# One LSTM step in TensorE's banks: input and bias rows injected behind the cell, twelve steps written out

## What the reference computes

```python
g0 = x[:, 0] @ W_ih[0].T + b_ih[0] + b_hh[0]
h, c = _lstm_activate(g0, c0)
def step(carry, x_t):
    h, c = carry
    sel_in = jnp.concatenate([h, c, x_t], axis=-1)
    logits = sel_in @ W_sel.T + b_sel
    onehot = jax.nn.one_hot(jnp.argmax(logits, axis=-1), Sx)
    g_all = einsum('bi,sgi->bsg', x_t, W_ih) + einsum('bh,sgh->bsg', h, W_hh) + b_ih + b_hh
    g = einsum('bsg,bs->bg', g_all, onehot)
    h2, c2 = _lstm_activate(g, c)      # sigmoid(f)*c + sigmoid(i)*tanh(g); sigmoid(o)*tanh(c2)
    return ((h2, c2), h2)
```

## Time and profile before

| | us |
|---|---|
| device time, median of 3 runs | 6272.86 (6269.54 to 6273.96) |
| the profiled execution, device time | 6278.15 |
| its span, first to last instruction | 6276.3 |
| PE busy | 5392.8 (86%) |
| DVE busy | 3097.9 (49%) |
| ACT busy | 1088.6 (17%) |
| POOL busy | 612.9 (10%) |

### The profile page before, as it was taken

One profiled execution on the slowest core, in us unless ns is written; L12 is line 12 of the kernel. 1 busy time (PEld: TensorE's weight loads), 2 busy tenths in 40 slices (PEclk: granted clock), 3 DMA queues, 4 the chain that ended last, 5 costly groups with the idle time before them and its releaser, 6 DMA issues. The chain is left out here.

```text
span 6276.3 us, 214043 instructions
## 1 busy us (share of the span) xinstructions
PE 5392.8 (86%) x84948; PEld 3269.5 (52%) x84948; DVE 3097.9 (49%) x13265; ACT 1088.6 (17%) x4645; POOL 612.9 (10%) x1014
## 2 busy tenths in 40 slices
PE   8998778849998929999999999999999999977778
PEld 6643443314666615555555555555555555544444
DVE  4401443214552165555555555555555555564543
ACT  0000000002331131111111111111111111122312
POOL 0000660002650000000000000000000000011100
PEclk9999998979999969999999999999999999989877
DMA  0000111467432330000000000000000000000010
GB/s 10 21 30 11 39 44 44 97 136 253 119 105 100 139 123 5 5 5 10 5 5 5 10 5 5 5 5 10 5 5 5 5 10 0 0 24 37 23 55 9
DMA packets 128787, 240.28 MB, mean 38 GB/s; under 512 B 47084, under 2 KB 64114, under 8 KB 127687
## 3 DMA queue, kind: packets, MB, share of 16 engines
q1 hardware_dynamic: 68584, 146.72, 6.6%
q0 software_dynamic: 60128, 92.58, 5.9%
HBM read 165.58 MB, written 73.29 MB: 38 GB/s over the span
## 5 line engine op out<-in xcount | busy, mean ns | idle before, releaser
L1456 PE MATMUL bank<-lstm_w,step_h_parts 128*32 128x128 f16 (+1 forms) x59904 | 1233.0, 238 | 172.1 <-issue 164.0
L1456 PEld LDWEIGHTS bank<-lstm_w,step_h_parts 128*32 128x32 f16 x59904 | 1116.8, 97 | 488.4 <-issue 478.0
L1427 PE MATMUL bank<-lstm_w 128*128 128x512 f16 x4992 | 1297.0, 383 | 3.2 <-issue 3.2
L1480 DVE TRANSPOSE_TENSOR_REDUCE step_summed<-bank 128x4 f32<-128x128 f32 x1872 | 670.0, 358 | 292.7 <-PE bank L1456 285.6
L1427 PEld LDWEIGHTS bank<-lstm_w 128*128 128x128 f16 x4992 | 386.4, 98 | 388.5 <-issue 5.1
L1406 ACT ACTIVATE step_act_out<-step_gates 128x4 f32<-128x4 f32 x625 | 128.5, 206 | 2082.3 <-DVE step_gates L1486 2078.8
L1486 DVE SCALAR_TENSOR_TENSOR step_gates<-step_summed,lstm_inv_scale,step_xgs 128x4 f32<-128x4 f32 x1872 | 416.0, 222 | 68.7
L1530 DVE COPY step_xgs<-step_xg 128x16 f32 x624 | 109.2, 175 | 688.7 <-issue 664.5
L1396 POOL COPY xnT<-step_state 128x4 f32 (+1 forms) x625 | 116.4, 186 | 3170.0 <-DVE step_state L1513 3170.0
L1109 PE MATMUL bank<-sum_parts,sum_hot 125*125 125x512 f16 x1600 | 347.6, 381 | 6.9 <-DVE sum_parts L1068 6.9
L1437 PE MATMUL bank<-lstm_wsel,step_state 128*1 128x4 f32 x4992 | 214.9, 168 | 115.3 <-DVE step_state L1503 115.3
(11 more groups left out here) (368 smaller groups left out, 6578.2 us busy)
## 6 DMA issues: line engine op xcount, KB each, us to landing
rel_h<-rel_h_sb SPq DMA_DIRECT2D x39, 1024.0 KB, 4.3
lstm_xg<-xg_g POOLq DMA_DIRECT2D x4, 5000.0 KB, 19.5
step_xg<-lstm_xg SPq DMA_DIRECT2D x25, 800.0 KB, 4.4
xg_w<-in_c_w_ih SPq DMA_DIRECT2D x8, 2048.0 KB, 10.7
lstm_w<-in_c_w_hh SPq DMA_DIRECT2D x4, 4096.0 KB, 30.8
rel_z<-rel_z_sb POOLq DMA_DIRECT2D x8, 1250.0 KB, 22.9
rel_zg<-rel_z POOLq DMA_DIRECT2D x8, 1248.0 KB
cheb_w<-in_L_gnn_weight SPq DMA_DIRECT2D x8, 1024.0 KB
```

The lines of the kernel that those rows point to most:

```text
L1427: nc.tensor.matmul(idle[:], w[:, 0, 0, 0, 0, 0:128], w[:, 0, 0, 0, 0, :], start=True, stop=True)
L1456: last = nc.tensor.matmul(bank[32 * q:32 * q + 32, 0:32 * (end - first)], h_parts[:, c, :], w[:, s, c, q, a, 32 * first:32 * end], start=( ...
L1480: nc.vector.tensor_reduce(summed[:, first:end], bank[:, 0:32 * (end - first)].rearrange("p (b r) -> p b r", r=32), X_AXIS, ALU.add, apply_ ...
```

## The change

Five things change, all in the LSTM.

1. `lstm_inputs` turns its products round: x is stationary (125 rows of x at a time), and 512 weight columns move. Each of 16 groups (gate and quarter of the hidden size) times 5 row tiles gives 80 tiles. The result is split into three bfloat16 parts (ACT takes the high and middle one, DVE the rests) and stored as `lstm_xg` with a bank's layout: 128 columns for each of the four cells. The bias is not added, but split and stored in the same way (`lstm_bias`).
2. In the loop, `inject` puts the input and bias rows of all four cells into each of four gate banks with one bfloat16 product of 512 columns (128 stationary columns). It stands at the start of the next step, right behind the cell's code, and waits for DVE's sum of that bank.
3. The cell has four parts of 128 columns (f, g, i, o) in place of three. It adds to the 128 columns of its cell in the injected bank. `add_input`, the copy `step_xgs` and the four `WARM_GATES` products are gone. ACT applies the scale while it reads the sums.
4. PE's loop has 52 rounds of 12 steps written out, so that a step's slot in the ring of input rows is a constant. DVE, ACT and POOL still loop over single steps.
5. DVE's wait for a part is `_wait_ge(done, 1)` on the reduction itself; four decrements behind the pick (`parts_taken`) bring the semaphores back to zero.

```diff
-WARM_PICK, WARM_GATES = 4, 4
+WARM_PICK = 4
-CHUNK = 25
-RING = 3 * CHUNK
+XG_CHUNK = 4
+XG_SLOTS = 3
+XG_RING = XG_SLOTS * XG_CHUNK
...
-                    wt = w[:, n % 2, c, i % (GC // 2), :]
-                    nc.tensor.matmul(B.bank[2 * (i % 4)][:, 0:CUT], wt, xnT[:, c, 0:CUT], start=(c == 0),
-                                     stop=(c == KC - 1))
-                    last = nc.tensor.matmul(B.bank[2 * (i % 4) + 1][:, 0:N - CUT], wt, xnT[:, c, CUT:N],
+                    last = nc.tensor.matmul(B.bank[i % 6][0:R, :], xnT[:, c, m * R:(m + 1) * R], w[:, n % 2, c, :],
                                             start=(c == 0), stop=(c == KC - 1))
...
-                act.wait_ge(gates_f, n)
-                nc.scalar.activation(act_out[:, 0:4], gates[:, 0:4], ACT.Sigmoid).then_inc(sig_f, 1)
+                act.wait_ge(summed_f, n)
+                nc.scalar.activation(act_out[:, 0:4], summed[:, 0:4], ACT.Sigmoid, scale=L.inv[:, 0:1]
+                                     ).then_inc(sig_f, 1)
...
-            with pe.Fori(1, STEPS) as t:
...
+            def inject(part, at, stop):
+                p, bank, _, _ = part
+                return nc.tensor.matmul(bank[:], rows[:, p, :], xg[:, at, :], start=True, stop=stop)
+
+            def add_half(part, s, c, a, stop):
+                p, bank, _, _ = part
+                for q in range(4):
+                    last = nc.tensor.matmul(bank[32 * q:32 * q + 32, 128 * s:128 * s + 128], h_parts[:, c, :],
+                                            w[:, s, c, q, a, 128 * p:128 * p + 128], start=False, stop=stop,
+                                            tile_position=(0, 32 * q))
+                return last
...
+            def step(t, at):
+
+                if at % XG_CHUNK == 0:
+                    pe.wait_ge(xg_loaded[at // XG_CHUNK], 16)
+                    pe.sem_inc(xg_loaded[at // XG_CHUNK], -16)
+                for part in parts:
+                    pe.wait_ge(part[3], t)
+                    last = inject(part, at, stop=False)
+                last.then_inc(injected, 1)
...
-                keep_clock_up(WARM_GATES)
+            with pe.Fori(0, ROUNDS) as r:
+                for at in range(XG_RING):
+                    step(pe.snap(r * XG_RING + (at + 1)), at)
...
-            def add_input(part, t):
-                first, end, _, _, summed_part, gates_part = part
-                dve.wait_ge(summed_part, t)
-                nc.vector.scalar_tensor_tensor(out=gates[:, first:end], in0=summed[:, first:end],
...
+                nc.vector.tensor_reduce(summed[:, 4 * p:4 * p + 4], bank[:, bass.ds(s * 128, 128)].rearrange(
+                    "p (b r) -> p b r", r=32), X_AXIS, ALU.add, apply_transpose=True
+                                        )._wait_ge(done, 1).then_inc(summed_part, 1)
```

More of the change, by code:

```diff
@@ L1178, in _, with take_rest @@
+            for k in range(4):
+                pool.wait_ge(stored[k], 16 * (TILES // 4))
         @block.vector
         def _(dve):
[L1180 to L1190, removed]
+            def take_rest(i):
+                if i >= 4:
+                    dve.wait_ge(lo_ready, i - 3)
+                dve.wait_ge(hi_ready, i + 1)
+                nc.vector.tensor_tensor(rest[:, i % 4], B.bank[i % 6][0:R, :], parts[:, i % 4, 0], ALU.subtract
+                                        ).then_inc(rest_ready, 1)
@@ L1196, in _, with keep_hi @@
         def _(act):
[L1197 to L1205, removed]
+            def keep_hi(i):
+                if i >= 4:
+                    act.wait_ge(stored[i % 4], 16 * (i // 4))
+                act.wait_ge(done, i + 1)
+                nc.scalar.copy(parts[:, i % 4, 0], B.bank[i % 6][0:R, :]).then_inc(hi_ready, 1)
@@ new lines, in lstm_steps @@
+    xg_loaded = [sem(f"xg_loaded{k}") for k in range(XG_SLOTS)]
+    w = L.raw[:, 0:BLOCKS, :].bitcast(F16).rearrange("p (s c q) (a k) -> p s c q a k", s=CELLS, c=KC, a=2)
+    part_f = (0, B.bank[0], done_f, summed_f)
+    part_g = (1, B.bank[1], done_g, summed_g)
+    part_i = (2, B.bank[2], done_i, summed_i)
+    part_o = (3, B.bank[3], done_o, summed_o)
+    parts = (part_f, part_g, part_i, part_o)
+    score = B.bank[4][0:1, 0:8]
+    idle = B.bank[5]
+    halves = [(c, a) for c in range(KC) for a in range(2)]
@@ L1449, in _ @@
                 s = pe.value_load(pick[0:1, 0:1])
-                def cell(s):
-                    for first, end, bank, done, _, _ in parts:
-                        for c in range(KC):
-                            for a in range(2):
-                                for q in range(4):
-                                    last = nc.tensor.matmul(
-                                        bank[32 * q:32 * q + 32, 0:32 * (end - first)], h_parts[:, c, :],
-                                        w[:, s, c, q, a, 32 * first:32 * end],
-                                        start=(c == 0 and a == 0), stop=(c == KC - 1 and a == 1),
-                                        tile_position=(0, 32 * q))
-                        last.then_inc(done, 1)
                 with pe.If(s < 2):
@@ L1555, in _ @@
             dve.wait_ge(init, 1)
-            dve.wait_ge(xg_loaded, 16)
-            for first, end, _, _, _, gates_part in parts:
-                nc.vector.tensor_copy(gates[:, first:end], xg[:, 0, first:end]).then_inc(gates_part, 1)
-            forget(1)
-            new_i(1)
-            new_c(1)
-            weigh_h(1)
-            new_h(1)
-            choose(1)
-            with dve.Fori(1, STEPS - 1) as t:
-                finish(t, t + 1)
-                choose(t + 1)
-            finish(STEPS - 1, STEPS)
+            dve.wait_ge(rows_loaded, 16)
+            nc.vector.tensor_scalar(rows[:], rows_f[:], L.up[:, 0:1], None, ALU.mult).then_inc(rows_ready, 1)
+            finish(0, None, 1)
+            with dve.Fori(1, STEPS) as t:
+                s = choose(t)
+                finish(s, t, t + 1)
 def add_hidden(nc, ctx, B, L):
@@ L2290, in lay_out @@
         b = out.pop("L2_ffn_" + name).reshape(4, 4, 4, 4, 32)[:, order]
[L2291 removed]
+        out["c_" + name] = np.ascontiguousarray(b.transpose(1, 2, 0, 3, 4).reshape(16, 512))
+    rows = np.zeros((128, 4, 128), np.float32)
+    for n in range(16):
+        rows[3 * n:3 * n + 3, n // 4, 32 * (n % 4)] = 1.0
+        rows[64 + 3 * n:64 + 3 * n + 3, n // 4, 32 * (n % 4)] = 1.0
+    out["c_xg_rows"] = rows
     w = out.pop("L2_ffn_W_sel")
```

233 lines of the change are left out of this document (139 added, 94 removed).

## The result

| | before | changed |
|---|---|---|
| device time, median, us | 6271.5 (6269.54 to 6273.96, 4 runs) | 11404.88 (11396.54 to 11422.4, 4 runs) |
| profiled span, us | 6276.3 | 11420.6 |
| mean granted clock of PE | 0.944 | 0.705 |

The changed kernel takes 1.8189 times as long, 95% interval 1.8157 to 1.822. The forecast was 10,540 us with a range of 8,900 to 12,300: the measured time lies inside it, 865 us above its middle.

What follows compares the result with a forecast made beforehand. The PE-DVE-ACT ring of the LSTM loop was taken as the bound, every wait paid 624 times. Step 4.55 + code arrival 6.2 + clock 1.2 = 12.0 us against 5.165: +4265 us, 10,540 us, range 8,900 to 12,300.

Steps and rivals of the forecast that it cites:

- The bound and its price: PE's instruction blocks in the LSTM loop: an absent one can be used 3.4 us after it is asked for.
- Rival 2: In the twelve-step loop, code stays or always arrives in time: 4.55 us a step, 5,900 us; chance 5%.
- The waits by cell: Waits for code at jumps and block edges in PE's loop, summed for each cell: mean 6.2 us a step.
- The jump to cell 3: Branch to the last cell copy in PE's loop: one jump of 772 instructions, 3.4 us.
- The step without the code's arrival: One LSTM loop step if no code had to arrive: 4.5 to 4.6 us, where it was 5.165.
- The four injects [...] lie where PE waits anyway: Injects in PE's loop: as long as the four `WARM_GATES` products they replace, 1.04 us, and placed where PE waits.
- The gain of 0.6 us in the new c: In the LSTM step the new c can start at about 4006.75 instead of 4007.35: 0.6 us less.
- The clock: PE's granted clock in the loop: low for over half the time, adding 1.2 us a step, bounds 0 and 1.9.
- The input stage: `lstm_inputs`: 640 passes in 272 us against 269 before, booked at 0, bounds -20 and +100 us.
- Rival 1: PE asks for two or three blocks ahead: 9.3 and 7.7 us a step, 8,860 and 7,860 us; chance 9%.
- rival 4: Gain and waits in the loop cancel, needing a mean wait of 0.6 us a step; chance 1%.
- Rival 3: A jump's block queues behind the next one already asked for: 11,790 to 12,350 us; chance 3% beyond the range.

Runs made afterwards that it cites:

- run 1: The kernel before with PE's step written out twelve times and nothing else changed but the place of the four filler products: 10409.07 us.
- run 4: The changed kernel with one step in PE's loop, the ring's slot from a register and one semaphore counting SP's loads: 6470.8 us, ratio 1.0313.
- runs 2 and 3: The kernel before with PE's step written out two times (6.5 blocks) and three times (9.8 blocks): 6285.08 us, ratio 1.001, and 11292.85 us.
- Run 7: The changed kernel with the four copies of the cell in reverse order in the code, branches turned to match: 11552.29 us, ratio 1.8406.
- run 5: The kernel of run 4 with the injects behind the scores, in place of three of the four filler products: 6264.52 us, ratio 0.9985.
- run 8: The kernel of run 5 with DVE's MAX8 and MAX_INDEX at its turn's end, value load and decrements at the next one's start: 6009.2 us, ratio 0.9577.
- Run 9: The kernel of run 8 with 8 instead of 4 buffers for the stores of the input stage: 5986.9 us, ratio 0.954.

## Why the prediction was right, and by how much it was off

**The bound and its price.** Right. The reading of the earlier trace rows, one jump that took 3605 ns and one pause within a cell, was the whole effect in small: a block that is not there costs PE 3.3 to 3.9 us at most jumps (3.4 was taken), and q8 moved 2425 packets (over 2000 forecast), 3.8 a step without the 45 of before (3 to 4). One reading was inexact: the clock fell at 2315.5 us, inside the gap that ended at 2316.31, and not behind it.

**The cause.** Shown. The old step written out has it without the rest of the change (run 1), and the change without the writing out does not have it (run 4). Rival 2, that the code stays, had its point in question at a loop of 51 blocks; runs 2 and 3 put the limit between 6.5 and 9.8.

**The waits by cell.** The prediction's waits for each cell, with its 4.55 us for the step and 1.2 for the clock added (5.75), stand beside what was measured from pick to pick:

| cell | predicted | measured | off by |
|---|---|---|---|
| 0 | 4.2 + 5.75 = 9.95 | 10.79 | 0.84 |
| 1 | 6.6 + 5.75 = 12.35 | 13.20 | 0.85 |
| 2 | 8.2 + 5.75 = 13.95 | 14.85 | 0.90 |
| 3 | 6.0 + 5.75 = 11.75 | 15.24 | 3.49 |

Two steps of the working failed, and they can be told apart here.

*The jump to cell 3* was booked as one jump of 772 instructions, 3.4 us. It is two: L1519 goes to the compare L1525, which stands ahead of cell 2, and that block has to arrive only to say that the next jump goes to cell 3, which has to arrive too. In the trace the first takes 3.61 us and the second 3.36 in the mean of the 129. That is the 5.83 us of idle time ahead of cell 3 in the timeline. 3.49 less the 0.86 that the other cells are off by as well is 2.6 us, times 129/624 = 0.54 us a step. Run 7 confirms it: the cell that stands last pays it, whichever it is.

*The step without the code's arrival* was booked at 4.55 us. Run 4 measured 5.43, and the 0.88 between them is what the other cells are off by. Both faults together, 0.88 + 0.54 = 1.42, are the 13.38 - 12.0 = 1.38 us by which the step was missed. In the 0.88 these things were wrong, in the order in which the runs took them away:
- "The four injects [...] lie where PE waits anyway": they stand between PE and the scores. This is the fault that the changed kernel shares. In run 4 the scores start 1.07 us after the new c. Moving the injects away gave 0.33 us a step (5.43 to 5.10, run 5), since another wait took over.
- That other wait is the order of DVE's loop, which was not costed: its branch and register work then stands between the new h and MAX8, 0.40 us (5.10 to 4.70, run 8). In run 4 and in the changed kernel it lies hidden behind the injects.
- 0.15 us are left in run 8. By the means over its steps the new c comes 0.55 us sooner after the pick is read than before the change (3.21 against 3.76 for cells 1 and 2), where 0.6 was booked, and MAX8 follows it 1.01 us later where it was 0.92. ACT's activations take 0.30 us now that they read the scale (L1447: 298 ns) where they took 0.21; that was not booked either. Whether that is the cause is not shown.

The gain of 0.6 us in the new c was right, and no part of it reaches the time of the change as made.

**The clock.** 0.64 in the loop, well under 1.0 as forecast. With levels of 2.4 and 1.2 GHz (1.0 and 0.5) that is the low one for 72% of the time (over half was expected). A cell's 128 products took 3.71 us at 2539.32 where they take 1.97 in run 4. In the loop PE is busy for 4231.63 us, where the same work takes 2841.22 at a clock of 1.00 (run 4). The 2.2 us a step between them are the most that the clock can have added to PE's own work, and part of them lies beside other waits. What it adds to a step can't be told apart from the waits in full. One part is free of them: from the first inject to the scores PE takes 1.1 to 1.4 us in the mean where it takes 0.96 in run 4. Less run 4's own step for the same cell (5.34, 5.47, 5.48 and 5.39 us), waits and clock together come to 5.45, 7.73, 9.37 and 9.85 us for cells 0 to 3, where 5.4, 7.8, 9.4 and 7.2 were booked.

For cell 0 that agreement is in part luck. From its last product to the next inject PE took 4.51 us in the mean, against 0.60 in run 4: 3.9 for a jump booked at 3.4. The rest of its step is 1.5 us longer than in run 4, where edge and clock were booked at 0.8 + 1.2 = 2.0.

**The input stage.** It was booked at 0 with bounds of -20 and +100 us. PE's loop starts at 2339.8, by the reading of the first pick, where it was 2308.2: +31.6 us. What is late are the stores: 80 transfers of 9.0 us, four at a time in flight, and ACT behind them for 204.5 us. Run 9 gives back 22 us.

**The rivals.** Rival 1 (several blocks ahead) and rival 4 (cancelled) fell by size. Rival 3 (queueing) gave from 11,790 up; the table of cells leaves no room for it in that size. A smaller delay of this kind may be there: the jumps from the ends of cells 0 and 1 took 4.03 and 3.96 us in the mean, and the branch that closes a round took 4.7 where a jump went just before it and 3.4 where none did. That such a jump waits behind a block already asked for was only argued.

By the rule of the Trainium skill ("Runtime: NRT & Kernel Launch", section "Instruction fetch mechanics") that the arrival is hidden in a straight run, the prediction's sum was 9,500 us. The pause of 1.52 us within cell 2's products, in the timeline at 2515.07, contradicts the rule here.

## What to carry to other kernels

Count the instructions of a loop before writing steps out: PE needs two for each product, and the price is not a share but a cliff. A loop of 6.5 blocks of 256 ran at full speed; one of 9.8 took 80% more time, and the one slow jump of the trace before, 3605 ns where 169 were usual, already had the price on it. Where code must be long, a tree of branches costs one more arrival for each compare that lies in a block of its own, so the commonest case goes first. Run 7 shows the sign of that: with the commonest cell, 195 of 624 steps, in the last place the kernel took 147 us more.

On a ring of engines, work put "where the engine waits anyway" must be checked against what the engine has to start next: four products of 0.26 us cost 0.33 us a step more ahead of the scores than behind them. A gain can stay hidden until the next wait is taken away too: DVE's loop end cost nothing while PE was late, and 0.40 us a step once PE was not.

## What the runs showed of the hardware that was not expected

- Two steps written out or one made no difference over 0.2% (ratio 1.001); three cost 80%. With three, PE loaded 11.5 blocks in each round of a loop of 9.8, not only the part above the limit.
- A jump to an absent block took 3.3 to 3.9 us at the median; a loop's closing branch with another such jump just ahead of it took 4.6 to 4.8, and without one 3.4 to 3.8.
- An activation with its scale read from SBUF took 298 ns for 128x4, where the same shape without it takes 0.21 us.
- A wait against a constant on the instruction itself, with a decrement later, was worth 0.18 us a step (0.13 to 0.22 by single runs) against four waits for the step number.
